# Causal attention on one core: where the pieces of a group's row maxima stand among the steps of the groups before it

## What is computed

```python
q, k, v = proj(wq, bq), proj(wk, bk), proj(wv, bv)      # 16 heads of 16
scores = jnp.einsum('bhqd,bhkd->bhqk', q, k) * scale
mask = jnp.triu(jnp.full((t, t), NEG, jnp.float32), k=1)
attn = jax.nn.softmax(scores + mask, axis=-1)
out = jnp.einsum('bhqk,bhkd->bhqd', attn, v)
```

## Time and profile before

| what | us |
|---|---|
| median of 3 runs | 2354.98 |
| lowest and highest | 2353.09, 2356.28 |
| profiled execution, its own time | 2356.39 |
| its span, first to last instruction | 2354.7 |
| first piece of the stage, last output turned (start) | 195.6, 768.0 |

### The profile page before, as it was taken

The page is one execution under the profiler, slowest core; times in us unless marked ns, Lnnn a source line. Parts: engine busy times, 40 slices in busy tenths (PEclk is TensorE's granted clock), DMA queues, the critical chain, the costliest instruction groups (busy, mean ns, idle before and its releaser), DMA issues.

```text
span 2354.7 us, 36114 instructions
## 1 busy us (share of the span) xinstructions
PE 2015.3 (86%) x11968; PEld 1253.7 (53%) x11968; DVE 1448.2 (62%) x3942; ACT 1241.8 (53%) x2980; POOL 798.6 (34%) x663
## 2 busy tenths in 40 slices
PE   5566899999988736989989989989989989989988
PEld 3232233333322525666666666656767667657666
DVE  5467677787774435646646746646745745746744
ACT  1121566666667224745754754753754754754663
POOL 2233221112232335505505505614613613613620
PEclk9796899999999868999999999999999999999999
DMA  5646744554530541000000000011100000000000
GB/s 145 153 132 134 141 98 66 82 82 69 103 109 10 158 138 77 1 28 10 1 23 14 1 23 14 1 66 64 49 19 19 19 19 18 19 4 33 19 1 27
DMA packets 124455, 128.97 MB, mean 55 GB/s; under 512 B 50460, under 2 KB 101232, under 8 KB 123248
## 3 DMA queue, kind: packets, MB, share of 16 engines
q1 hardware_dynamic: 123696, 117.75, 21.6%
q0 software_dynamic: 576, 8.91, 1.0%
HBM read 75.51 MB, written 50.86 MB: 54 GB/s over the span
## 4 chain that ended last, share of the span: by engine, by line
PE 35%; DVE 13%; ACT 8%; issue 6%; POOL 2%; DMA 0%; DVEq 0%; SPq 0%; POOLq 0%; ACTq 0%
DVE rot_s L1862 5%; PE qkv_ps L1372 5%; PE s_ps L1412 4%; PE qkv_ps L1313 4%; PE s_ps L1359 3%; PE pt_ps L1425 3%; PE s_ps L1493 3%; PE o_ps L1450 3%; DVE p_sb L1871 3%; ACT p_sb L1605 2%; POOL inv_norm L1756 2%; PE pt_ps L1412 2%; PE o_ps L1412 2%; PE pt_ps L1493 2%; PE o_ps L1493 2%
## 5 line engine op out<-in xcount | busy, mean ns | idle before, releaser
L699 ACT ACTIVATE probs<-st_ps 128x512 f32<-128x512 f32 (+3 forms) x768 | 327.9, 495 | 185.9 <-PE st_ps L614 184.4
L1313 PE MATMUL qkv_ps<-w_qkv,x_parts 128*128 128x512 f32 x1152 | 309.2, 412 | 33.4 <-DVE x_parts L1836 24.1
L744 DVE CUSTOM_DVE_ANT_0 seen<-s_ps,causal 128x128 f32<-128x128 f32 (+3 forms) x512 | 234.8, 485 | 90.1 <-PE s_ps L599 89.9
L1605 ACT ACTIVATE p_sb<-p_sb,negmax 128x256 f32<-128x256 f32 (+1 forms) x512 | 249.5, 490 | 71.4 <-DVE negmax L1871 71.1
L599 PE MATMUL s_ps<-k_stack,q_stack 96*128 96x512 bf16 (+3 forms) x768 | 244.7, 348 | 42.0 <-DVE piece_negmax L744 20.5
L1313 PEld LDWEIGHTS qkv_ps<-w_qkv,x_parts 128*128 128x128 f32 x1152 | 212.0, 194 | 81.2 <-issue 39.5
L614 PE MATMUL st_ps<-q_stack,k_stack 98*128 98x512 bf16 (+3 forms) x768 | 235.1, 337 | 19.0 <-ACT probs L699 14.4
L1871 DVE CUSTOM_DVE_ANT_0 p_sb<-s_ps,band 128x256 f32<-128x256 f32 (+1 forms) x512 | 185.5, 401 | 89.9 <-PE s_ps L1359 85.2
L1621 ACT COPY p_t<-pt_ps 128x512 f32<-128x512 f32 (+1 forms) x256 | 143.6, 561 | 162.5 <-PE pt_ps L1425 161.1
L821 POOL TENSOR_SCALAR_AFFINE_SELECT probs<-probs 128x512 f32<-128x512 f32 x128 | 81.6, 637 | 433.0 <-ACT probs L699 433.0
L1764 POOL TENSOR_TENSOR rot_c<-qn,turn_by 128x512 f32<-128x512 f32 x128 | 178.6, 1415 | 137.8 <-PE turn_ps L1339 111.9
(11 more groups left out here) (146 smaller groups left out, 3505.1 us busy)
## 6 DMA issues: line engine op xcount, KB each, us to landing
qk_scratch<-parts SPq DMA_DIRECT2D x64, 192.0 KB, 2.8
q_stack<-qk_scratch SPq DMA_DIRECT2D x96, 128.0 KB, 6.7
k_stack<-qk_scratch SPq DMA_DIRECT2D x96, 128.0 KB, 7.1
w_ffn<-ffn_weights POOLq DMA_DIRECT2D x4, 2176.0 KB, 11.7
v_scratch<-v_out SPq DMA_DIRECT2D x32, 256.0 KB, 2.6
v_sb<-v_scratch SPq DMA_DIRECT2D x16, 512.0 KB, 10.0
x_in<-xt_scratch SPq DMA_DIRECT2D x16, 512.0 KB, 4.1
ffn_weights<-w_high SPq DMA_DIRECT2D x2, 2176.0 KB, 7.6
```

The source lines that it names most:

```text
L699: act.activation(probs[:, n % 3, h, q0:CH], st_ps[i % 3][:, q0:CH], ACT.Exp).then_inc(exp_done.sem, 1)
L744: dve.tensor_tensor_reduce(seen[:, i % 3, 0:kw], s_ps[i % 3][:, 0:kw], causal[:, CH - kw:CH], -1.0, BIG, ALU.add, ALU.min, result).then_in ...
L1313: mm = pe.matmul(qkv_ps[:, part * CH:(part + 1) * CH], x_parts[:, w % XR, xp, k, :], w_qkv[:, wp, k, part * INNER:(part + 1) * INNER], sta ...
L1605: act.activation(p_sb[:, u % 4, h, k0:PW], p_sb[:, u % 4, h, k0:PW], ACT.Exp, scale=-1.0, bias=negmax[:, u % 4, h:h + 1], accum_out=total[ ...
```

## The change

The pieces become one stream over all groups. `beside` begins its walk at step `TURN` = 48 - 8 = 40, goes on to step 47 and then from 0 to 39, with 1.03 instead of 1.08 times the columns. In steps 40 to 47 of a group the pieces are those of the second next group (`behind(following)`), in steps 0 to 39 the rest of the following group's. `STARTED` is the number taken in the last eight steps, five. `first` makes these five for group 1 as well, behind the 48 of group 0. `PIECES_AT` is now

```diff
+TURN = NS * HG - 8
+
 def beside():
     columns = [CH - first_query(*SETS[n]) for n in range(NS) for h in range(HG)]
-    pieces, shift, taken, upto, i = [], {}, 0, 0, 0
-    for at, cols in enumerate(columns):
-        upto += cols * 1.08
+    pieces, shift, taken, upto, i = [0] * (NS * HG), {}, 0, 0, 0
+    for at in list(range(TURN, NS * HG)) + list(range(TURN)):
+        upto += columns[at] * 1.03
         first = i
...
-        pieces.append(i - first)
+        pieces[at] = i - first
     return pieces, shift
 
 PIECES_AT, SHIFT_AT = beside()
+STARTED = sum(PIECES_AT[TURN:])
...
+        def behind(group):
+            if group in (None, (B - 1, SLOTS - 1)):
+                return None
+            r, s = group
+            return r + (s + 1) // SLOTS, (s + 1) % SLOTS
...
                 shift_rows(group, 1)
+                loaded(behind(group))
+                for i in range(STARTED):
+                    score_piece(behind(group), i)
                 pe.wait_ge(shift_ones, 1)
 
             def group_work(group, previous, following):
-                if following:
-                    loaded(following)
-                piece = 0
+                piece = STARTED
                 for i in range(NS * HG):
                     n = i // HG
                     shifted_score(group, i)
+                    if i == TURN:
+                        piece = 0
+                        if behind(following):
+                            loaded(behind(following))
+                    target = following if i < TURN else behind(following)
+                    if target:
+                        for _ in range(PIECES_AT[i]):
+                            score_piece(target, piece)
+                            piece += 1
                     if following:
-                        for _ in range(PIECES_AT[i]):
-                            score_piece(following, piece)
-                            piece += 1
                         if i in SHIFT_AT:
...
             def first(group):
                 for i in range(NP * HG):
                     reduce_piece(group, i)
+                for i in range(STARTED):
+                    reduce_piece(behind(group), i)
 
             def group_work(group, previous, following):
-                piece = 0
+                piece = STARTED
                 for i in range(NS * HG):
-                    if following:
+                    if i == TURN:
+                        piece = 0
+                    target = following if i < TURN else behind(following)
+                    if target:
                         for _ in range(PIECES_AT[i]):
-                            reduce_piece(following, piece)
+                            reduce_piece(target, piece)
                             piece += 1
```

## The result

The kernel after takes 2338.83 us (median of seven runs, 2336.29 to 2346.52), the kernel before 2356.28 (seven runs on the same chips, 2351.86 to 2360.44): ratio 0.9935, 95% interval 0.9916 to 0.9953, so between 11 and 20 us saved, 15.3 by the ratio and 17.5 by the medians. Faster, as forecast, and inside the range; but about half of the 32 us that the forecast gave. The execution that was profiled took 2343.6 us with a span of 2341.9; the profiled pair differ by 12.8.

The account below looks back on a forecast made before the run. Waits from where the pieces stand, not a full engine, were taken as the bound. Twelve groups at 2.1 us (25.2) plus 6.6 in groups 1 and 13 made 31.8 us saved, giving 2323 us, range 2309 to 2342.

Parts of the forecast that it names:

- Rival (a): Whole kernel: reordering pieces only moves waits, VectorE's work stays, period 32.86, 2355 us; chance 0.08.
- sets 0 to 11: A group's 48 steps, four per set; their terms sum to 2.15 us saved, taken as 2.1 in twelve groups.
- my replay: PE's order worked through from trace prices, set by set; claimed error 0.1 us a set, 0.9 over nine.
- sets 3 to 5: Steps 12 to 23: the join precedes set 5's six pieces, VectorE reaches set 6 no earlier; 0.1 us lost.
- sets 10 and 11: Steps 40 to 47: five added pieces and the second turning at step 40, PE waiting 0.4 us; 0.15 lost.
- Groups 1 and 13: Groups that also split the feed-forward weights: 3.3 us saved in each, 6.6 together.
- the 1.8 for the hold: Groups 1 and 13: the earlier join is held while PE and VectorE wait anyway; 1.8 us saved each, between 0 and 3.4.
- 1.5 each for sets 7 to 9: Groups 1 and 13, steps 28 to 39: 1.5 us saved in each group.
- Group 0: First group: any saving is waited out at group 1's first score, which stays at 260 behind the shift rows; 0 gained.
- The signs I had named: Trace checks: period 30.8 us, wrong above 32; VectorE gap under 1; ScalarE idle 1.4 and 0.7 before sets 8 and 9.
- (b): Step 40: PE waits 1.3 to 1.4 us for the join, ScalarE runs dry; 0.9 a group slower, 2368 us; chance 0.06.
- (c): Full groups: uniform load lets ScalarE run near the group without pieces; over 3.0 us a group, 2300 or less; chance 0.06.

Follow-up runs that it names:

- the placing alone: Kernel before with only the factor 1.08 changed to 1.03, pieces kept within the group ahead: 2362.1 us against 2357.55, ratio 1.0019.
- the stream alone: Kernel after with the old factor 1.08, so only the eight-step turn of the pieces remains: 2351.38 us, ratio 0.9962 to before.
- the other placement: Kernel after with pieces per step from a search, nine lent instead of five, turnings at steps 20 and 42: 2305.55 us, ratio 0.9779.
- the kernel with the loads and copies moved: The other placement plus stack 3's load behind group 1's shift rows, ScalarE's weight copies spread singly, weights' stores later: 2287.97 us, ratio 0.9700.
- the last version: The kernel with the loads and copies moved, plus the second weights' load behind group 12's last shift rows: 2286.09 us, ratio 0.9706 to before.

## Why the prediction was right in sign and half in size

**What bounded the kernel: right.** The order of the pieces sets the period, and no engine's work fills it. It is shown from both sides: an unchanged amount of work goes through in 32.86, 31.89, 31.38 or 29.31 us by order alone, 4.8 us more of ScalarE's cost 0.05, and 6.25 us more of VectorE's cost 2.76, so of the engines it is VectorE's time that reaches the period, by less than half. Rival (a), that nothing moves, is out: VectorE busy for 79% of a group left at least 3.55 us to be had, without a change to its work. The rule that I had set beside it (the Trainium skill, "Perfetto Trace Analysis", Identifying the Most-Contended Engine: the engine of highest occupancy first) named the right engine, since longer VectorE work costs and longer ScalarE work does not, but does not tell what order can give.

**The sum over sets 0 to 11: the direction of each term right, each of them too favourable, the sum 2.15 instead of 0.97.** By set starts of group 6:

| sets | forecast | measured |
|---|---|---|
| 0 to 2 | -0.4 | -0.27 |
| 3 to 5 | +0.1 | +0.42 |
| 6 | -0.6 | -0.43 |
| 7 | -0.35 | -0.16 |
| 8 | -0.7 | -0.66 |
| 9 | -0.35 | -0.22 |
| 10, 11 | +0.15 | +0.35 |

Two steps failed.

The first is the sentence "my replay errs by 0.1 a set, so over nine sets by 0.9 either way". It does not err either way. Of the lengths that I had replayed for after each was too short: set 6 2.9 against 3.09 measured, set 7 3.8 against 4.02, set 8 2.95 against 3.00, set 9 2.1 against 2.19, 0.55 together. (That a replay leaves out small things that all cost time, such as a queue's hand-over, is my reading; no run takes them one by one.) In sets 6, 7 and 9 I set the replay of after against the *measured* before, and each error went into the gain. A full replay of all twelve sets by the same prices, made afterwards for both kernels, gives 31.7 for before and 30.6 for after; both are too short, by 1.16 and 1.29, and their difference of 1.1 is near the 0.97 measured. In part that is luck: the same replay was short by 1.58 for the placing alone (31.1 against 32.68 in its shortest groups), by 0.88 for the stream alone (31.7 against 32.58) and by 1.61 for the other placement (27.7 against 29.31). It was too fast all five times, but by 0.9 to 1.6, so that its differences to after are off by 0.3 to 0.4 us. The lower bound of 0.9 a group held just so.

The second is the term "sets 3 to 5: minus 0.1". I saw that the join now precedes all six pieces, and wrote that VectorE "reaches set 6 no earlier". What I missed is that PE fills its ring of three during the join, then stands in front of a piece with a score behind it. Set 5 went from 3.69 to 4.20; with the join two pieces later it is 3.77, with the turning one step later 3.96. Both pieces of the cause are thus measured: 0.43 and 0.24, which is more than the 0.51 lost, so they overlap; no run has both. In sets 10 and 11 the second turning costs: 0.28 come back when it stands a step later, of the 0.35 lost. Of the 1.18 missing in a group, 0.53 are in sets 6 to 9, 0.32 in sets 3 to 5, 0.20 in sets 10 and 11, and 0.13 in sets 0 to 2, for which no run was made.

**Groups 1 and 13: 6.6 forecast, 1.26 measured.** The failed term is the 1.8 for the hold, between "0 (held again later)" and 3.4. The lower end was what happened: COPY, CAST and the last TENSOR_TENSOR are held one after another by successive subtractions of GpSimd, so the join takes 6.26 us, and two runs with the subtraction cut show that the hold costs 6.33 after and 6.48 before. The other term, 1.5 each for sets 7 to 9, failed too: 1.1 for both groups. The Trainium skill's "SBUF — State Buffer" (Terms, shared port pair), by which the loser blocks for the whole instruction, agrees with the 2.35 and 2.40 us of the two rows. What I took from it, that the join would be through about 5 us after the first subtraction, counted the hold as over once the CAST had passed; the last TENSOR_TENSOR is held anew, since the next subtraction is already there. It also put that end one microsecond behind ScalarE's copies; by the earlier trace rows it would have been two (275.27 and 5 against 274.11 and 4.09), and in group 13 of after it was 4.5. GpSimd's timeline in group 13 of after has the four subtractions:

```profile
665.03 9.82 POOL L836 TENSOR_TENSOR w_raw<-w_raw,w_high 128x1088 fp32r<-128x1088 f32 x4 [0.15 <-ACT w_high L730]
```

At 2.46 each the first three end at 667.5, 669.9 and 672.4, and these are, within 0.1, the ends of COPY (667.54), CAST (670.00) and the last TENSOR_TENSOR (672.43): 7.4 us after 665.03, not 5.

**Group 0: 0 forecast, 1.3 less by period, 0.5 by group 1's first score.** PE's timeline in after:

```profile
259.68 0.61 PE L625 MATMUL st_ps<-q_stack,k_stack 98*128 98x512 bf16 x1 [2.24 <-DMA q_stack<-shift_sb]
```

It comes at 259.68 (260.16 before) after a wait for the shift rows: what group 0 gained was waited out there but for 0.5. The rows that this score waits for are the first half's, issued behind the loads at 240.50 and 241.06 (241.16 and 241.72 before) and 18.4 us under way by their median (17.9 before); the second half's, issued near 255, take under 5, and the median of 11.1 in the earlier trace rows lies between the two. That the first pair is issued 0.66 earlier is the 0.5 that I had at 0. The 0.9 us by which the five pieces in front of group 0 push its start is waited out there too. Behind this wait PE's granted clock was 0.53 over ten microseconds:

```profile
260.38:270.38 10.00, 10.00 (x46) 3.15 (x44) 6.12 (x20) 5.83 (x13) 1.27 (x2) 0.53 0.01 2
```

So a slow clock stands at the head of group 1 as well, which takes 2.8 us more than group 13; how much of that is the clock's was not measured. In the placed version this wait is still 2.08 (at 260.82); with the fourth stack's load behind the shift rows it is gone.

**The signs I had named.** VectorE's gap before group 7 is 0.64 (under 1: yes), its busy time in group 6 26.30 (26.0 forecast), ScalarE's before set 8 is 1.43 (near 1.4: yes), before set 9 0.94 (near 0.7: no), PE's wait for the join at step 40 is 0.35 (0.4 forecast), PE's timeline shows no wait for a stack's load at step 40, and the gap on ScalarE after the copies is 2.89 (not over 1.5: wrong). The period of 31.89 is just under the 32 that I had named as the limit of "wrong". Rivals (b) and (c) did not occur; (c) was open for another placement, though not for this one.

## What to carry to other kernels

When a change reorders work between engines that are coupled by short rings, compare replay with replay, never a replay with a measured time: the errors of this replay had one sign, and only a difference cancels the most of them. Even so it was off by 0.3 to 0.4 us of 32, as much as some of the edits brought. In such a replay a handful of tiny instructions in front of a full ring counts as a stop of the whole chain for its length, and moving it behind two pieces, or the consumer one step later, can bring half as much as the large move (0.4 and 0.5 us of 32 here, against 0.97 for the whole change). Small transfers that the next stage waits for go into the queue ahead of any large load, and a chain of tiny VectorE instructions in SBUF stays clear of back-to-back long GpSimd instructions.

## What the runs showed of the hardware that I had not expected

- Four VectorE instructions that take 0.66 us in all took 6.26 beside GpSimd's subtractions (2.46 us each, four in a row). Each of COPY, CAST and the last TENSOR_TENSOR was held until a subtraction ended (in group 13 of before it was COPY and the first TENSOR_TENSOR, 2.52 us), and the maxima read from PSUM were not: 0.28 to 0.69 us at the same time.
- A wait on PE was followed by more loss than itself. In the set that began 1.98 us behind the end of 1.65 us idle the granted clock was 0.63 (the placing alone). Behind 2.32 us idle it was 0.66 over ten microseconds (group 12 of the kernel with the loads and copies moved), behind 2.24 us 0.53 (group 1 of after), and behind 3.24 and 2.91 us idle 0.50 and 0.56 over ten microseconds (group 13 of after), where a score of 512 columns took 0.63 instead of 0.39.
- Over the first ten microseconds of group 0 the granted clock was 0.57 in two executions (placed, and the last version) and 0.88 in one, with the same or nearly the same program ahead of it: 2.7 us of difference in group 0 that no edit explains. What decides when it rises was not tried.
